# Unify stage: products of chunk n+2 ahead of the transposes of chunk n, rows normalised in place, router's parts formed in this stage

## What is computed

```python
    x = x + _L0_attn_ref(xn, ...) + _L0_ffn_ref(xn, ...)      # attention ends with: out @ W_unify + b_unify
    xn = _layernorm(x, axis=-1)
    x = x + _L1_attn_ref(xn, ...) + _L1_ffn_ref(xn, ...)
    # _L1_attn_ref: y = _rmsnorm(xn, norm_w); y_conv (3 taps) + conv_b; scan h = tanh(a) * h + b * y
    # _L1_ffn_ref:  logits = relu(xn @ rw1 + rb1) @ rw2 + rb2; top 2 of 8; experts on the chosen rows
```

## Time and profile before

| | |
|---|---|
| median of 3 runs | 3974.03 us |
| lowest, highest | 3969.38, 3999.69 us |
| the run that was profiled | 3956.84 us |
| span of its profile | 3955.0 us |
| TensorE busy over the span | 3784.0 us (96%) |
| VectorE busy | 3306.2 us (84%) |
| ScalarE busy | 2727.7 us (69%) |
| GpSimd busy | 453.2 us (11%) |

### The profile page before, as it was taken

One profiled execution on the slowest core, in us unless ns is written; L12 is line 12 of the kernel. 1 busy time (PEld: TensorE's weight loads), 2 busy tenths in 40 slices (PEclk: granted clock), 3 DMA queues, 4 the chain that ended last, 5 costly groups with the idle time before them and its releaser, 6 DMA issues. The chain is left out here.

```text
span 3955.0 us, 84753 instructions
## 1 busy us (share of the span) xinstructions
PE 3784.0 (96%) x31366; PEld 1957.8 (50%) x31366; DVE 3306.2 (84%) x3515; ACT 2727.7 (69%) x4939; POOL 453.2 (11%) x402
## 2 busy tenths in 40 slices
PE   8799899999999999999999999999997859999998
PEld 6587333333333333333333333333334538888887
DVE  6567799999899999989999999999973837766664
ACT  2454688888788888878888888888885422223332
POOL 0133200000000000000000000000002225002323
PEclk9899999999999999989999999999998979999999
DMA  4811331122022122112202112201113011005332
GB/s 140 234 28 22 105 36 21 12 26 28 11 25 33 10 23 26 20 14 25 29 9 31 29 10 26 33 10 7 10 31 83 1 52 59 1 2 148 77 78 38
DMA packets 301759, 158.58 MB, mean 40 GB/s; under 512 B 218397, under 2 KB 273507, under 8 KB 298800
## 3 DMA queue, kind: packets, MB, share of 16 engines
q1 hardware_dynamic: 289072, 142.49, 18.9%
q0 software_dynamic: 12288, 10.70, 1.6%
HBM read 86.46 MB, written 64.18 MB: 38 GB/s over the span
## 5 line engine op out<-in xcount | busy, mean ns | idle before, releaser
L1210 ACT ACTIVATE probs<-attention_scores_t_sums 128x512 f32<-128x512 f32 x4096 | 2217.3, 597 | 313.6 <-PE attention_scores_t_sums L1134 96.9
L1244 DVE TENSOR_REDUCE max_parts<-attention_scores_q_sums 128x1 f32<-128x1024 f32 x1008 | 1223.8, 1222 | 53.2 <-PE attention_scores_q_sums L1128 46.3
L1244 DVE TENSOR_REDUCE attention_max_parts<-attention_scores_q_sums 128x1 f32<-128x1024 f32 x992 | 1207.4, 1224 | 16.7 <-PE attention_scores_q_sums L1128 9.2
L1134 PE MATMUL attention_scores_t_sums<-q_operand,k_operand 50*128 50x512 f32 x2048 | 767.3, 454 | 14.3 <-ACTq L1224 14.0
L1134 PE MATMUL attention_scores_t_sums<-attention_q_operand,attention_k_operand 50*128 50x512 f32 x2048 | 751.3, 445 | 0.0
L1128 PE MATMUL attention_scores_q_sums<-attention_k_operand,attention_q_operand 48*128 48x512 f32 x2048 | 745.1, 443 | 0.0
L1128 PE MATMUL attention_scores_q_sums<-k_operand,q_operand 48*128 48x512 f32 x1952 | 726.2, 452 | 5.2 <-issue 5.2
L1143 PE MATMUL attention_o_psum_sums<-probs,v_heads 128*32 128x256 f32 x8192 | 667.4, 398 | 2.0 <-ACT o_parts L1206 0.2
L1143 PE MATMUL attention_o_psum_sums<-probs,attention_v_heads 128*32 128x256 f32 x8208 | 655.8, 391 | 1.9
L1128 PEld LDWEIGHTS attention_scores_q_sums<-attention_k_operand,attention_q_operand 48*128 48x128 f32 x2048 | 301.4, 184 | 421.8 <-DVE attention_max_parts L1244 188.6
L1128 PEld LDWEIGHTS attention_scores_q_sums<-k_operand,q_operand 48*128 48x128 f32 x1952 | 293.7, 188 | 421.3 <-DVE attention_max_parts L1244 177.1
(11 more groups left out here) (322 smaller groups left out, 4620.7 us busy)
## 6 DMA issues: line engine op xcount, KB each, us to landing
o_other_half<-o_parts SPq DMA_DIRECT2D x130, 64.0 KB, 2.0
expert_rows<-attention_empty_rows SPq DMA_DIRECT2D x16, 516.0 KB, 5.7
v_scratch<-value_chunk SPq DMA_DIRECT2D x16, 512.0 KB, 4.9
w_whole<-in_L_ffn_ew SPq DMA_DIRECT2D x8, 1024.0 KB, 6.9
experts_w_whole<-in_L_ffn_ew SPq DMA_DIRECT2D x8, 1024.0 KB, 5.7
q_operand<-q_scratch SPq DMA_DIRECT2D x24, 256.0 KB, 4.9
...
```

Source lines behind the costliest of these rows:

```text
L1134: nc.tensor.matmul(ST[bank_n][:, :], KOP[b][64 * h:64 * h + ROWS + 2, kt * P:(kt + 1) * P], QOP[b][64 * h:64 * h + ROWS + 2, c * CH:(c + 1 ...
L1210: nc.scalar.activation(PR[:, tile, :], ST[bank_n][:, :], ACT.Exp).then_inc(st_free, 1)
L1244: nc.vector.tensor_reduce(MPART[par][:, h, u // 4, u % 4:u % 4 + 1], SA[h][:, :], AX.X, ALU.max)\
```

## The change

Four things are changed. On TensorE, `unify(n + 2)` stands ahead of `turn(n, 0)`. VectorE writes the normalised rows straight into `XN1` (function `rows(n)`); `XG` and GpSimd's copies are gone, and transposes and `YG` read `XN1`. VectorE's reciprocal of the last denominators stands behind `add(0)` and `variances(0)`, and `added` counts it there (`sums(n)`). The router's weights and its chunk 0 are split inside the unify stage: the loads are issued behind chunk 5's, ScalarE forms both high parts behind its copies of chunk 5 (n == NCH - 3), GpSimd both low parts behind chunk 7's multiplication; VectorE's `split` of the weights is gone from the router phase.

```diff
...
@@ -1339,12 +1338,18 @@
         TP = [ph.ps(f"norm_transposed{k}") for k in range(2 * KC)]
         den_in, recip_out = ph.sem("denominators_in"), ph.sem("recip_den_and_tokens")
         at_ready, u_ready, added, var_ready, root_ready = (
-            ph.sem(n) for n in ("edges_set", "unified_ready", "recip_den_done_then_attention_added",
+            ph.sem(n) for n in ("edges_set", "unified_ready", "attention_added_and_recip_den_done",
                                 "variances_ready", "roots_ready"))
-        EDGES, RECIPS = 2, 1
-        xg_ready, yg_ready, n_ready, n_copied, xn_kept = (
-            ph.sem(n) for n in ("xn_ready", "y_ready", "norm_transposed_ready", "norm_copied", "xn_kept"))
+        EDGES, RECIPS = 2, 2
+        xg_ready, yg_ready, n_ready, n_copied = (
+            ph.sem(n) for n in ("xn_ready", "y_ready", "norm_transposed_ready", "norm_copied"))
         block = ph.block()
+
+        def sums(n):
+            return 1 if n == 0 else n + 2
+
+        def rows(n):
+            return XN1[:, n * TC:(n + 1) * TC, 0:C]
 
         @block.sync
         def _(sp):
@@ -1368,7 +1373,8 @@
                 outs.load_rows(sp, att_scratch, n)
                 sp.wait_ge(outs.normal, n - 1)
                 outs.load_recips(sp, recip_scratch, n)
-            load_router(sp)
+                if n == 5:
+                    load_router(sp)
             sp.wait_ge(recip_out, 48)
 
         @block.gpsimd
@@ -1378,18 +1384,19 @@
             pool.wait_ge(at_ready, 1)
             nc.gpsimd.memset(YT[:, :, T + 1:T + 2], 0.0).then_inc(at_ready, 1)
             pool.wait_ge(at_ready, EDGES)
-            for n in range(NCH):
-                pool.wait_ge(xg_ready, n + 1)
-                nc.gpsimd.tensor_copy(XN1[:, n * TC:(n + 1) * TC, 0:C], XG[n % 2][:, :, :]).then_inc(xn_kept, 1)
-                if n + 4 < NCH:
-                    outs.normalise(nc, pool, n + 4)
+            for n in range(4, NCH):
+                outs.normalise(nc, pool, n)
+            pool.wait_ge(router.high_ready, 1)
+            nc.gpsimd.tensor_tensor(router.W1[1][:, :, :], router.whole, router.W1[0][:, :, :].bitcast(F32), ALU.subtract)\
+                .then_inc(router.w_split, 1)
+            router.low(nc, pool, XT1, 0, 0)
 
         @block.tensor
         def _(pe):
             def unify(n):
                 pe.wait_ge(outs.normal, n + 1)
                 if n >= 2:
-                    pe.wait_ge(added, RECIPS + n - 1)
+                    pe.wait_ge(added, sums(n - 2))
                 for j in range(TC):
                     for q in range(KC):
                         mm = nc.tensor.matmul(UP[n % 2][j // 2][:, j % 2 * C:(j % 2 + 1) * C], AT[n % 4][:, q, j * P:(j + 1) * P],
@@ -1402,7 +1409,7 @@
                     if n:
                         pe.wait_ge(n_copied, (n - 1) * 2 * KC + g * KC + m + 1)
                     for j in range(TC):
-                        mm = nc.tensor.transpose(TP[g * KC + m][:, j * P:(j + 1) * P], src[n % 2][:, j, m * P:(m + 1) * P],
+                        mm = nc.tensor.transpose(TP[g * KC + m][:, j * P:(j + 1) * P], src[:, j, m * P:(m + 1) * P],
                                                  CST[:, IDENT:IDENT + P])
                     mm.then_inc(n_ready, 1)
 
@@ -1410,10 +1417,10 @@
             unify(0)
             unify(1)
             for n in range(NCH):
-                turn(n, 0, XG, xg_ready)
                 if n + 2 < NCH:
                     unify(n + 2)
-                turn(n, 1, YG, yg_ready)
+                turn(n, 0, rows(n), xg_ready)
+                turn(n, 1, YG[n % 2], yg_ready)
 
         @block.scalar
         def _(act):
...
@@ -1442,6 +1449,11 @@
                         act.wait_ge(at_ready, EDGES)
                     nc.scalar.activation(YT[:, m, n * CH + 1:(n + 1) * CH + 1], TP[KC + m][:, :], ACT.Copy,
                                          scale=NW[:, m:m + 1]).then_inc(n_copied, 1)
+                if n == NCH - 3:
+                    act.wait_ge(router.w_in, router.w_total)
+                    nc.scalar.copy(router.W1[0][:, :, :], router.whole).then_inc(router.high_ready, 1)
+                    act.wait_ge(n_copied, 2 * KC)
+                    router.high(nc, XT1, 0, 0)
 
         @block.vector
         def _(dve):
@@ -1475,18 +1487,15 @@
                 if n >= 2:
                     dve.wait_ge(yg_ready, n - 1)
                 link(nc.vector.reciprocal(RECIP[k][:, :, :], ROOT[k][:, :, :]))
-                if n >= 2:
-                    dve.wait_ge(xn_kept, n - 1)
-                    dve.wait_ge(n_ready, (n - 2) * 2 * KC + KC)
                 for j in range(TC):
-                    ins = nc.vector.tensor_scalar(XG[k][:, j, :], X[:, n * TC + j, :], MV[k][:, j, 0:1],
+                    ins = nc.vector.tensor_scalar(rows(n)[:, j, :], X[:, n * TC + j, :], MV[k][:, j, 0:1],
                                                   RECIP[k][:, 0, j:j + 1], ALU.subtract, ALU.mult)
                 ins.then_inc(xg_ready, 1)
 
-            dve.wait_ge(den_in, 32)
-            nc.vector.reciprocal(RD[:, :], DEN[:, :]).then_inc(added, RECIPS)
             add(0)
             variances(0)
+            dve.wait_ge(den_in, 32)
+            nc.vector.reciprocal(RD[:, :], DEN[:, :]).then_inc(added, 1)
             for n in range(NCH):
                 if n + 1 < NCH:
                     add(n + 1)
@@ -1505,16 +1514,27 @@
         self.W1 = [sb(f"router_w1_{part}", [P, KC, HID], F32R) for part in ("high", "low")]
         self.XN = [[sb(f"router_xn_{part}{k}", [P, KC, CH], F32R) for k in range(2)] for part in ("high", "low")]
 
-    def parameters(self, sb, links):
+    def high(self, nc, XT1, n, k):
+        nc.scalar.copy(self.XN[0][k][:, :, :], XT1[:, :, bass.ds(n * CH, CH)]).then_inc(self.high_ready, 1)
+
+    def low(self, nc, pool, XT1, n, k):
+        pool.wait_ge(self.high_ready, n + 2)
+        nc.gpsimd.tensor_tensor(self.XN[1][k][:, :, :], XT1[:, :, bass.ds(n * CH, CH)], self.XN[0][k][:, :, :].bitcast(F32),
+                                ALU.subtract).then_inc(self.xl_ready, 1)
+
+    def parameters(self, sb, sem, links):
+        self.high_ready, self.xl_ready, self.w_split = (sem(n) for n in ("router_w_then_xn_high_ready", "router_xn_low_ready",
+                                                                         "router_parts_cleared_weights_split"))
         self.W2, self.B1, self.B2 = sb("router_w2", [P, MH, E1]), sb("router_b1", [P, MH]), sb("router_b2", [P, E1])
         self.CW = sb("conv_w", [P, KC, 3])
         three = sb("conv_b_a_b", [P, 3, KC])
         self.CB, self.AV, self.BV = (three[:, n, :] for n in range(3))
         self.RH = sb("router_hidden", [P, 4, CH])
+        self.whole = self.RH[:, :, :].rearrange("p (k a) c -> p k (a c)", k=KC)
         self.w_in, self.w_total = links.inputs, links.expect(8)
 
     def load(self, sp, rw1, rb1, rw2, rb2, conv_w, conv_b, a, b):
-        sp.dma_start(self.RH[:, :, :].rearrange("p (k a) c -> p k (a c)", k=KC), rw1.rearrange("(k p) n -> p k n", p=P))\
+        sp.dma_start(self.whole, rw1.rearrange("(k p) n -> p k n", p=P))\
             .then_inc(self.w_in, 16)
         for dst, src in ((self.CB, conv_b), (self.AV, a), (self.BV, b)):
             sp.dma_start(dst[:, :], src.rearrange("(k p) -> p k", p=P), allow_slow_non_contiguous=True).then_inc(self.w_in, 16)
@@ -1534,25 +1554,20 @@
                                           router.RH)
         S = AV
         L4 = RH[:, 3, :]
-        W1 = RH[:, :, :].rearrange("p (k a) c -> p k (a c)", k=KC)
         HP = [ph.ps(f"hidden{k}") for k in range(3)]
         LP, SUM_P = ph.ps("logit_parts"), ph.ps("logits")
         h_ready, r_done, l4_copied, s_ready, l_copied = (
             ph.sem(n) for n in ("hidden_ready", "relu_done", "logit_parts_copied", "logits_ready", "logits_copied"))
-        w_split, xh_ready, xl_ready, l_unit = (ph.sem(n) for n in ("parts_cleared_weights_split",
-                                                                          "xn_high_ready", "xn_low_ready",
-                                                                          "logit_unit_done"))
-        decay_ready = ph.sem("decay_ready")
+        l_unit, decay_ready = ph.sem("logit_unit_done"), ph.sem("decay_ready")
+        w_split, xl_ready = router.w_split, router.xl_ready
         block = ph.block()
 
         @block.gpsimd
         def _(pool):
-            with pool.Fori(0, NCH // 2) as i:
+            router.low(nc, pool, XT1, 1, 1)
+            with pool.Fori(0, NCH // 2 - 1) as i:
                 for k in range(2):
-                    n = 2 * i + k
-                    pool.wait_ge(xh_ready, n + 1)
-                    nc.gpsimd.tensor_tensor(XL[k][:, :, :], XT1[:, :, bass.ds(n * CH, CH)],
-                                            XH[k][:, :, :].bitcast(F32), ALU.subtract).then_inc(xl_ready, 1)
+                    router.low(nc, pool, XT1, 2 * i + 2 + k, k)
 
         @block.tensor
         def _(pe):
...
@@ -1641,7 +1652,6 @@
 
```

(1 more changed line is left out.)

14 lines of the change are left out of this document (5 added, 9 removed).

## The result

| | before | changed |
|---|---|---|
| median | 3977.95 us (13 runs) | 3958.85 us (13 runs) |
| lowest, highest | 3968.59, 3999.69 | 3948.48, 3966.76 |
| ratio, changed to before | | 0.9942, 95% interval 0.9929 to 0.9955 |
| second comparison, taken later | 3945.22 (30 runs) | 3929.25 (10 runs), ratio 0.9956, interval 0.9937 to 0.9974 |

The changed kernel is faster by 0.58% (first comparison) or 0.44% (second), 17 to 23 us by the ratios; the medians themselves differ by 19.1 and 16.0 us. The forecast was 22, and 3952 us for the median. Between the two comparisons the kernel before differs from itself by 33 us, so only kernels timed beside each other are compared.

What follows compares the result with a forecast made beforehand. Bound: a TensorE-VectorE ring, 9.45 us per chunk, before the router's first product (3091.33). Moving that to 3067.0 gives 24.3 us, less 1.7 (half clock) and 0.6 (contention): 22, so 3952 from the median; range 3930 to 3968.

Steps and rivals of the forecast that it cites:

- rivals A: Unify stage: a late chunk 6 (3 us) and two more half-clock stretches (3.4) leave 16 us, 3958; chance 0.14.
- E: Unify stage: GpSimd holds up the normalising of chunk 7 by 1.8 to 4.1 us; gain 19 us, 3955; chance 0.10.
- Part 1: TensorE's products(n+2) ahead of chunk n's transposes: cycle 5.7 us, was 9.45; products(4) at 3029.4 in place of 3042.06.
- Part 2: VectorE's last reciprocal behind add(0) and variances(0): rows(0) some 4 us earlier, no further gain at the end.
- Part 3: GpSimd's eight copies disappear, VectorE normalises into rows 258 apart at 409 ns a piece: worth about 0.
- Part 4: Router's 8 loads issued before rows 6 and 7: chunk 6 there at 3037.9 to 3041.2, wanted 3040.8; delay taken as 0.
- Part 5: Weights' split leaves the router's entry: gain 5.3 us; ScalarE's casts add 3.1 on the path; first router product 3067.0.
- The wait of L1467: VectorE's tiny TENSOR_SCALAR took 1.68 in place of 0.17 during GpSimd's multiplication; such waits, on chunks 3 and 4, counted 0.6 us.
- the forecast's own sign of being wrong: Unify stage: L1482's counterpart, VectorE's normalising, at 2 us beside GpSimd would show the lock; the forecast took 0.
- Half clock: TensorE in the unify stage: one more stretch at 1.2 GHz than the steps hold, counted as 1.7 us.
- Rival B: TensorE stays at 1.2 GHz throughout the unify stage: 2 us slower, router's first product 3093.3, 3976; chance 0.03.
- Rival D: Behind the router's start: no change, a later stage waits for something with a time of its own; chance 0.03.

## Why the prediction was right, and where it was not

- **Place and size.** That 3091.33 moves by 22 us, and the time by 0.55%: T fell by 16.8 and 18.1 in the two profiles, the time by 17 to 23 us. The median and the range held it. The T of the profiles is 4 to 5 us short of the 22, at the low end of the forecast's own 17 to 27 (16.8 lies just under it) and nearer to what rivals A (16) and E (19) gave. That the first comparison's 23 lies so near 22 is luck.
- **Part 1, right.** Products(4) were put at 3029.4; counted from the first product as before, they started at 3006.04 + 23.46 = 3029.50. This needs Part 2 as well: with the order alone they started at 3006.04 + 26.86 = 3032.9. So the 12.7 us of that run are not the 12.7 by which the forecast has chunk 4 earlier (3042.06 to 3029.4): 9.2 come from chunk 4, the rest from the chunks behind it.
- **Part 2, right in what it does, wrong in its price.** The forecast says both that the end gains nothing of it and that it lets the early chunks be done by then. The second is what counts: without the edit T was 3.6 to 5.0 us longer. The sum was not touched, since products(4) were timed with the edit in.
- **Part 3.** No gain was forecast for the copies. No run took them alone; Parts 3 to 5 together brought 0.5 (72.6 to 72.1). A normalising into the rows 258 apart took 1.38, as before.
- **Part 4, nearly right.** Chunk 6 was put at 3037.9 to 3041.2 (its low end is 0.5 too early: 3031.4 + 0.9 + 3.7 is 3036.0, not 3035.5). It was there at 3041.8 by the same count, since SyncE needed 10.2 us for the eight issues in place of 7.9, and TensorE waited 0.75; putting the loads back changed nothing that can be measured.
- **Part 5, and the waits for GpSimd: the step that failed.** The entry to the router was right: 0.99 after the last copy (1.03 forecast), a gain of 5.5. ScalarE's casts took 1.92 and 1.07, 3.0 in all (3.1). But the router's first product, put at 3067.0, came at 3060.22 + 14.36 = 3074.6, 7.6 late, where the forecast had taken off 2.3. The lateness grew at three places, all of them locks. Rows(3) were 2.1 late, behind the normalising of chunk 2 (4.56). Rows(4) were 5.9 late, behind chunk 4's variances (1.67 and 2.04 of waiting). ScalarE's casts ended 4.0 late; then `root(7)` stood 4.62 for chunk 7's variances (3.8 and 1.9), and rows(7), expected at 3060.2, came at 3054.42 + 14.36 = 3068.8, 8.6 late. I had looked for GpSimd's two subtractions only in ScalarE's and TensorE's path ("end by 3063, inside this") and not at VectorE's. Of the 5.3 that the entry gave, nothing was left, as the run with the split put back shows.
- **Contention, named and undersized.** The wait of L1467 was read from the rows and charged to chunks 3 and 4, "where VectorE has 2 us to spare", with 0.6 us. It did fall on chunk 4, but on two operations (3.7 us together), and the spare was gone, since the normalising of chunk 2 had made VectorE 2 us late. TensorE waited 2.00 for these rows. And it fell on chunk 7.
- **The normalising, wrong; rival E was right in kind.** I argued from 409 ns in place of half of it that the normalising needs nothing of GpSimd's. It does wait: 4.56, 4.59, 3.40 and 2.35 us for four pieces that take 1.38 alone, and one piece 2.44, which is the forecast's own sign of being wrong ("at 2 us beside GpSimd"). But rival E looked for it in chunk 7; in the changed kernel it came in chunk 2, and what waited in chunk 7 were the variances. In the ten profiles 21 pieces of 256 columns began beside a TENSOR_TENSOR of GpSimd, and every one ended 0.15 us behind it. By L1649's 2343 ns for 4096 columns, 256 columns would need 0.146 us, an estimate; so most of the 409 ns is no time per column, and a piece's duration says nothing of whether it takes the lock. Here the two pages of the Trainium skill that the prediction cites held, "SBUF — State Buffer" (SBUF: two separate sides) for the lock, and the rule that tensor_scalar of fp32 in SBUF is among the operations concerned ("VectorE: DVE Perf Modes", The perf-mode tier table).
- **Half clock.** The tail ran at it from chunk 6's second transposes (1.97), as the steps allowed for. Rival B did not come: six groups of products ran at 3.62 to 4.32. Rival D did not either: behind the router's first product the second profile of the changed kernel takes 862.1 us, before 863.7.
- **Why the total came right all the same:** the stage lost 4 to 5 us more than was taken off the sum (24.3 less 2.3, against 16.8 and 18.1). The first timed comparison (0.9942, 23 us) gives back more than T shows, the second (0.9956, 17 us) as much. I can't say more of the difference than that the two intervals overlap.
